# Sparsemax attention with a Fourier layer: the check of the thresholds is summed by rank on TensorE, ahead of the next keys

## What is computed

```
def sparsemax(x):
    zs = -jnp.sort(-x, axis=-1); cssv = jnp.cumsum(zs, axis=-1) - 1.0
    support = zs > cssv / rho
    k = jnp.maximum(jnp.sum(support, axis=-1, keepdims=True), 1)
    tau = jnp.take_along_axis(cssv, k - 1, axis=-1) / k
    return jnp.clip(x - tau, 0.0)
scores = jnp.einsum('bhqd,bhkd->bhqk', qh, kh) * scale
out = jnp.einsum('bhqk,bhkd->bhqd', sparsemax(scores), vh)
```

## Time and profile before

| | us |
|---|---|
| median of 3 runs | 724.58 |
| lowest and highest of them | 724.3, 726.02 |
| the profiled execution, its own time | 725.45 |
| its span, first to last instruction | 723.7 |
| TensorE busy (matmuls) | 584.8 |
| VectorE busy | 609.3 |
| ScalarE busy | 380.7 |
| GpSimd busy | 187.1 |

### The profile page before, as it was taken

One profiled execution on the slowest core, in us unless ns is written; L12 is line 12 of the kernel. 1 busy time (PEld: TensorE's weight loads), 2 busy tenths in 40 slices (PEclk: granted clock), 3 DMA queues, 4 the chain that ended last, 5 costly groups with the idle time before them and its releaser, 6 DMA issues.

```text
span 723.7 us, 14347 instructions
## 1 busy us (share of the span) xinstructions
PE 584.8 (81%) x4560; PEld 332.5 (46%) x4560; DVE 609.3 (84%) x2964; ACT 380.7 (53%) x657; POOL 187.1 (26%) x239
## 2 busy tenths in 40 slices
PE   3785989798814998899899998990889988997575
PEld 1343545454402654565455544550445544655242
DVE  5699799977966999999999999994899999999600
ACT  3664565766611755666566646560456665563321
POOL 2511403241220240415033502351014430301301
PEclk9879978999965999999999999996899999996857
DMA  9752131202220113130303030303102111200000
GB/s 315 237 166 72 27 103 47 59 0 71 68 76 0 28 28 101 33 84 15 110 26 95 6 105 28 106 1 84 42 1 78 39 45 31 59 17 14 11 1 11
DMA packets 33471, 44.23 MB, mean 61 GB/s; under 512 B 8353, under 2 KB 26785, under 8 KB 33382
## 3 DMA queue, kind: packets, MB, share of 16 engines
q1 hardware_dynamic: 32332, 41.16, 20.0%
q10 hardware_dynamic: 1056, 2.10, 0.8%
HBM read 23.77 MB, written 1.64 MB: 35 GB/s over the span
## 4 chain that ended last, share of the span: by engine, by line
PE 64%; issue 16%; ACT 11%; DVE 4%; SPq 3%; DMA 1%; POOL 1%; POOLq 0%; DVEq 0%
PE ring L456 33%; PE ring L522 8%; PE ring L545 5%; PE ring L599 5%; PE mix_bank L570 5%; PE ring L495 4%; PE ring L507 3%; ACT qst L674 2%; ACT S L674 2%; SPq L248 2%; ACT ctx L674 1%; DMA S<-in_L_xattn_Wk 1%; SPq L252 1%; ACT v L674 1%; ACT ks L682 1%
## 5 line engine op out<-in xcount | busy, mean ns | idle before, releaser
L929 DVE MAX8 cand<-S 100x8 f32<-100x45 f32 (+1 forms) x2048 | 223.1, 188 | 0.5 <-issue 0.4
L456 PE MATMUL ring<-wv,ctx 128*121 128x512 f16 x576 | 156.7, 392 | 0.0
L456 PE MATMUL ring<-ctx,wk 128*128 128x361 f16 x768 | 136.1, 339 | 4.5 <-DVE ctx L1108 4.5
L798 ACT ACTIVATE pT<-ring 121x800 f32<-121x800 f32 x96 | 80.5, 839 | 75.2 <-PE ring L599 75.2
L674 ACT ACTIVATE S<-ring 100x722 f32<-100x722 f32 x128 | 95.2, 774 | 27.6 <-PE ring L545 27.2
L456 PEld LDWEIGHTS ring<-ctx,wk 128*128 128x128 f16 x768 | 78.9, 104 | 58.6 <-issue 14.9
L333 POOL TENSOR_TENSOR ctx<-ctx_f,ctx 128x484 f16<-128x484 f32 x42 | 50.6, 1205 | 163.8 <-ACT ctx L674 163.4
L545 PE MATMUL ring<-kst,qst 96*100 96x361 f16 x256 | 68.0, 361 | 29.4 <-ACT S L674 12.9
L456 PEld LDWEIGHTS ring<-wv,ctx 128*121 128x121 f16 x576 | 71.8, 137 | 33.4 <-issue 7.9
L599 PEld LDWEIGHTS ring<-qst,kst 99*121 99x121 f16 x768 | 61.5, 150 | 45.5 <-issue 21.7
L341 POOL TENSOR_TENSOR ks<-k_f,ks 128x361 f16<-128x361 f32 x64 | 57.2, 894 | 90.9 <-ACT k_f L686 88.2
(11 more groups left out here) (126 smaller groups left out, 727.3 us busy)
## 6 DMA issues: line engine op xcount, KB each, us to landing
kst<-ks SPq DMA_DIRECT2D x384, 45.1 KB, 1.9
ctx_f<-in_ctx SPq DMA_DIRECT2D x45, 242.0 KB, 2.9
xq<-in_x SPq DMA_DIRECT2D x8, 200.0 KB
xr<-in_x SPq DMA_DIRECT2D x8, 200.0 KB
out_y<-att SPq DMA_DIRECT2D x8, 200.0 KB
S<-in_L_xattn_Wk ACTq DMA_DIRECT2D x1, 1024.0 KB, 6.8
wq<-in_L_xattn_Wq ACTq DMA_DIRECT2D x1, 1024.0 KB, 11.3
wcos<-in_L_ffn_theta SPq DMA_DIRECT2D x1, 1024.0 KB, 10.4
```

The lines of the kernel that those rows point to most:

```text
L456: last = nc.tensor.matmul(psum, lhs(c, i), w(c, j), start=(c == 0 and n == 0), stop=(c == DC - 1 and n == 2))
L798: nc.scalar.activation(pT[0:CK, u % 3, :, :], src, ACT.Relu).then_inc(two_read, 1)
L929: last = nc.vector.max(cand[:, h, 8 * n:8 * n + 8], S[0:L, HH * (i % 2) + h, cuts[n]:cuts[n + 1]])
```

## The change

It changes how the flags are made, where they are summed, and how they are read.

- `thresholds`: the last step is held at zero or above, so that counts can't rise; the five instructions of lines 969 to 979 are replaced by one comparison of all 8 x 16 x 8 candidates with tau, written to `over` by rank (16-bit, the ranks 128 elements apart).
- `sum_flags`: nine matmuls in place of two: `n_over` times ones, and for each rank its 128 marks times -1 (ranks one to seven) or +1 (the eighth), into 8 x 17 places of partition 0. It stands behind `scores(i+1)` in phase i, in even phases ahead of `o_of(b-1)`, no longer between the key groups of phase i+1.
- `read_flags` for `rank_flags`: a sum over the 17 places of each head, a comparison times 2^h, and a sum to one word; behind three heads in place of four. `settle` stands behind four heads in place of five, loads the word once, and finds the flagged heads by shifts and tests in three nested loops of two.
- the first `maxes` of a half waits for `flag_ready` of the half before.

```diff
-                pe.wait_ge(flag_ready, i + 1)
-                nc.tensor.matmul(flag_ps, ones[:, :], n_over[:, :], start=True, stop=False)
-                nc.tensor.matmul(flag_ps, minus[:, :], n_now[:, :], start=False, stop=True).then_inc(flag_sum, 1)
+                pe.wait_ge(flag_ready, i + 1)
+                nc.tensor.matmul(flag_ps[:, :, PIECES], ones[:, :], n_over[:, :], start=True, stop=True)
+                for r in range(8):
+                    last = nc.tensor.matmul(flag_ps[:, :, 0:PIECES], (one_b if r == 7 else minus_b)[:, :],
+                                            by_rank[:, r, :, :], start=(r == 0), stop=(r == 7))
+                last.then_inc(flag_sum, 1)
...
                         run(k_of(b + 1, 0, 0), 4)
                         run(k_of(b + 1, 1, 0), 4)
-                    if attended:
-                        sum_flags(i - 1)
...
                     weave(heads, fill, 1)
+                    if i < NH:
+                        sum_flags(i)
                     if b > 0:
                         run(o_of(b - 1), 4)
...
             def maxes(i, h):
                 dve.wait_ge(two_read, seen2(("s", i, h)))
+                if h == 0 and i > 0:
+                    dve.wait_ge(flag_ready, i)
...
+                nc.vector.scalar_tensor_tensor(t, step_t[:, :], 0.0, t, ALU.max, ALU.add).then_inc(tau_ready, 1)
                 dve.wait_ge(tau_ready, i + 1)
-                counted(nc.vector.tensor_tensor(marks[:, :, :, 7:8], pieces[:, :, :, 7:8],
-                                                t4.broadcast_to([L, HH, PIECES, 1]), ALU.is_lt))
...
+                nc.vector.tensor_tensor(by_rank.rearrange("p r g n -> p g n r"), pieces, t4.broadcast_to([L, HH, PIECES, 8]), ALU.is_ge).then_inc(flag_ready, 1)
...
+                nc.vector.reduce_sum(lost[:, :], flag_ps, AX).then_inc(check_step, 1)
+                dve.wait_ge(check_step, 1)
+                nc.vector.scalar_tensor_tensor(code[:, :], lost[:, :], 0.5, bit_c[:, :],
                                                ALU.is_gt, ALU.mult).then_inc(check_step, 1)
...
+                    nc.vector.reduce_sum(word_i[:, :], code[:, :], AX).then_inc(check_step, 1)
...
-                    with dve.Fori(0, HH // 2) as pair:
-                        leading = dve.value_load(ranked_i[0:1, bass.ds(2 * pair, 1)], min_val=0, max_val=HH)
...
+                    with dve.Fori(0, 2) as four:
+                        with dve.If(((word >> (4 * four)) & 15) > 0):
+                            with dve.Fori(0, 2) as pair:
+                                with dve.If(((word >> (4 * four + 2 * pair)) & 3) > 0):
+                                    with dve.Fori(0, 2) as k:
+                                        with dve.If(((word >> (4 * four + 2 * pair + k)) & 1) > 0):
+                                            refine(i, 4 * four + 2 * pair + k)
...
                     found = maxes(i, h)
+                    if h == 2 and i > 0:
+                        read_flags(i - 1)
                     if h == 3 and i > 0:
-                        rank_flags(i - 1)
-                    if h == 4 and i > 0:
                         settle(i - 1)
```

More of the change, by code:

```diff
@@ L148, in build_kernel @@
         dif, over = sb("dif", [L, HH, NCAND]), sb("over", [L, HH, NCAND], BF16)
-        fold = sb("fold", [L, HH, 2 + NCAND // 2], BF16)
+        fold = sb("fold", [L, HH, 2 + PIECES * max(RANKS) // 2], BF16)
         tau = sb("tau", [L, 2, HH])
[L151 to L154, removed]
+        f_sum, step_t, n_over = (sb(n, [L, HH]) for n in ("f_sum", "step_t", "n_over"))
+        zero = sb("zero", [L, 1])
+        one_b, minus_b = sb("one_b", [L, 1], BF16), sb("minus_b", [L, 1], BF16)
+        bit_c, code, lost = (sb(n, [1, HH]) for n in ("bit_c", "code", "lost"))
+        word_i = sb("word_i", [1, 1], I32)
         again, againT = sb("again", [P, 32]), sb("againT", [P, 32])
@@ L164, in build_kernel @@
         mask_row = over[:, :, :].rearrange("p g n -> p (g n)")[:, 0:N]
+        by_rank = over[:, :, :].rearrange("p g n -> p (g n)").rearrange("p (r g n) -> p r g n", r=8, g=HH)
         s_flat = S[:, :, :].rearrange("p h n -> p (h n)")
@@ L962, in thresholds @@
                     after(n)
-                    last = nc.vector.scalar_tensor_tensor(t, step_t[:, :], STRETCH[turn], t, ALU.mult, ALU.add)
                     if turn < len(RANKS) - 1:
-                        n = counted(last)
-                last.then_inc(tau_ready, 1)
+                        n = counted(nc.vector.scalar_tensor_tensor(t, step_t[:, :], STRETCH[turn], t, ALU.mult, ALU.add))
+                nc.vector.scalar_tensor_tensor(t, step_t[:, :], 0.0, t, ALU.max, ALU.add).then_inc(tau_ready, 1)
                 dve.wait_ge(tau_ready, i + 1)
-                marks = over[:, :, :].rearrange("p g (n r) -> p g n r", r=8)
-                counted(nc.vector.tensor_tensor(marks[:, :, :, 7:8], pieces[:, :, :, 7:8],
-                                                t4.broadcast_to([L, HH, PIECES, 1]), ALU.is_lt))
[L971 to L980, removed]
+                nc.vector.tensor_tensor(by_rank.rearrange("p r g n -> p g n r"), pieces, t4.broadcast_to([L, HH, PIECES, 8]), ALU.is_ge).then_inc(flag_ready, 1)
             def two_steps(t):
@@ L1012, in test_sums, with refine @@
                 dve.wait_ge(fix, 3 + P // 32)
-            def refine(i, number):
-                number = nc.s_assert_within(number, 1, HH, skip_runtime_bounds_check_because="inside If(number > 0)")
-                t = tau[:, i % 2, bass.ds(number - 1, 1)]
-                row = S[0:L, bass.ds(number - 1 + HH * (i % 2), 1), :].rearrange("p a n -> p (a n)")
+            def refine(i, h):
+                h = nc.s_assert_within(h, 0, HH - 1, skip_runtime_bounds_check_because="a sum of three bits")
+                t = tau[:, i % 2, bass.ds(h, 1)]
+                row = S[0:L, bass.ds(h + HH * (i % 2), 1), :].rearrange("p a n -> p (a n)")
                 dve.sem_clear(fix)
@@ L1052, in rank_flags @@
                                                ALU.is_gt, ALU.mult).then_inc(check_step, 1)
-                dve.wait_ge(check_step, 1)
-                nc.vector.max(ranked[:, :], code[:, :]).then_inc(check_step, 1)
                 dve.wait_ge(check_step, 2)
-                nc.vector.tensor_copy(ranked_i[:, :], ranked[:, :]).then_inc(check_step, 1)
+                with nc.allow_low_precision(reason="a sum of distinct powers of two under 256"):
+                    nc.vector.reduce_sum(word_i[:, :], code[:, :], AX).then_inc(check_step, 1)
@@ L1058, in settle @@
             def settle(i):
                 dve.wait_ge(check_step, 3)
[L1060 to L1061 removed]
+                word = dve.value_load(word_i[0:1, 0:1], min_val=0, max_val=2 ** HH - 1)
+                with dve.If(word < 1):
                     dve.sem_inc(verified, 1)
[L1063 removed]
+                with dve.If(word > 0):
                     dve.wait_ge(tau_split, i + 1)
[L1065 to L1071 removed]
+                    with dve.Fori(0, 2) as four:
[5 more added lines that the diff above has]
+                                            refine(i, 4 * four + 2 * pair + k)
```

25 lines of the change are left out of this document (9 added, 16 removed).

## The result

| | before | after |
|---|---|---|
| median, us (4 runs each, same chip) | 724.44 | 755.40 |
| lowest and highest | 722.93, 726.02 | 755.08, 756.05 |
| span of the profiled execution | 723.7 | 753.3 |

The ratio is 1.0428, 95% interval 1.0405 to 1.0452: **31 us slower**, far outside my range (721.5 to 731.0).

The account below looks back on a forecast made before the run. The prediction took TensorE to set the pace, with GpSimd's split close behind. Its terms, from +4.1 for the sum to -3.6 and -1.8 for finding heads, summed to +2.0 us on 724.58: 726.6, range 721.5 to 731.0.

Parts of the forecast that it names:

- VectorE's marks: In thresholds, one comparison of 1024 elements takes 1.9 us, with the new wait 1.95 in place of 3.18; almost none shows.
- s: VectorE's time saved per half by the new comparison: 1.2 us, between 0.8 and 1.7.
- B: Rival: slower, TensorE stands in front of the keys in every even half; 730.7 us at a 3.0 us comparison; chance 0.14.
- The place: Sum ahead of the keys: a new TensorE wait in half 4, +2.2 us, and +0.84 at the end.
- added nothing: Slow first keys after odd phases at low granted clock: flags take some of this stretch in place of keys, 0 us.
- TensorE's sum: Nine matmuls in place of two on TensorE: 0.37 us more per half, in eleven halves +4.1.
- Finding the heads: Head tests in the refined halves, 0.6 us less each: -3.6 in half 10, -1.8 in half 3.
- One head earlier: Earlier reading and settling: nothing without refinement; -0.2 us in half 3, +0.84 in half 10, cut off by GpSimd's split.
- The end: Last halves: flags ahead of o_of(6) +0.84 us, VectorE's saving -1.2, the last sum +0.37.
- A: The forecast's own mechanism holds: 724.2 to 728.9 us; chance 0.62.
- C: Rival: faster, the nine matmuls cost TensorE next to nothing, -2.3 us; 723.3 or 721.5 with further savings; chance 0.19.
- D: Rival: the flagged set changes, a refined half costing 18 to 27 us; about 700 or 745 us; chance 0.05.

Follow-up runs that it names:

- added comparisons: The changed kernel with seven forms of the comparison added at its end, twice each; kernel 768.67 us in its one run.
- the two kernels with the 2.0 us comparison: The changed kernel with the comparison's loops turned, ranks outermost: 735.83 us with the sum at the new place, 727.11 us with it back between the key groups.
- the fastest: The kernel before with the word of bits and the flags read behind three heads, settled behind four; sum at its old place: 718.20 us, ratio 0.9923.
- the quick comparison: The changed kernel with only the comparison's loops turned, ranks outermost, so the same marks are written in runs: 735.83 us, ratio 1.0142.
- both undone: The changed kernel with the sum put back between the key groups and the comparison's ranks outermost, the rest kept: 727.11 us, ratio 1.0034.
- the doubled ones: The kernel with both undone, its eight matmuls by rank run twice in each half: 741.64 us, ratio 1.0227.

## Why the prediction was wrong, point by point

**The step that failed: VectorE's marks.** I put s = +1.2 us per half, between 0.8 and 1.7; it is 3.18 - 4.77 = **-1.6**. The row that could tell stood in the earlier trace rows: line 969 writes its marks singly, eight apart. I took its start to start, 0.35 us for 128, called the scaled 2.8 us too high, and gave line 971 its full 1.30. Both run into one another, and the start of the next instruction isn't the end of the last one's writes. The two together take 187.62 + 1.30 - 187.27 = 1.65 us; line 971's share at the pace of natural order (1.22 us per 1024) is 1.07; 0.58 is left for line 969, 4.5 ns per mark, as in the change. The added comparisons bear this out: the same 128 marks alone take 0.72 us there, of which 0.15 is fixed by the line through the three least times (an estimate; each form ran twice, and the shorter two took longer the first time). Its own duration, 0.73 us for 128, scales to 5.8, an upper bound that I hadn't used: I had kept 2.3 as the upper end of the range. The rule of the Trainium skill that the prediction names ("Advanced Engine Details and Errata", "SBUF Cachelines") spoke against the layout, and the trace agrees; I had let it cost 0.4.

**The rival that came true is B**, at 4.7 us in place of 3.0: TensorE stands in front of its next work. It was not every even half, as I had it (1, 3, 4, 7, 12, 13), I think because VectorE, late itself, and the slow keys shift against each other. By B's own rule, two savings less per even half without a wait, 4.7 us would have given some 4.0 in each of four halves and 2.8 twice: 748. Its mechanism would have been enough for three quarters of the loss; I gave it 0.14.

**The place was under-priced** even with quick marks: 8.1 us on the kernel before, 8.7 between the two kernels with the 2.0 us comparison, 11.4 on the fastest (5 to 10 at equal clock). Mine came to about 3. What I had set to nothing is the clock. I had seen that it is low behind odd phases, and "added nothing", since the flags would take some of the slow stretch in place of keys. They don't: with the quick comparison the eight matmuls of odd halves 1 to 13 come 102 to 106 ns apart at the new place and 58 at the old one, 3 us in sum, and the keys take 2 more in sum, not less. And with the sum at this place there are stretches at the lower level where there were none, in `attend` above all (14.0 to 17.1 us). On the kernel before, whose marks aren't quicker, the lower clock in `attend` is 4.1 of the 8 us and the waits in halves 4, 8 and 10 are 3.3.

**TensorE's sum** (0.84 with its hole, 0.37 more per half): near, at the full clock. From the hole to the next keys it takes 0.93 in half 0, with 59 ns per matmul against my 57; in the seven halves at the lower level it is 0.43 more; the page "TensorE: Matmul & The Clock Gate" of the Trainium skill, section "Back-to-back issue gap", has about 81 ns for such a stream, which this trace doesn't show. The kernel with both undone is 8.9 us above the fastest, where 16 times 0.44 (its 48 keys with the sum among them take 7.95 us against 7.51) gives 7.0. I had counted eleven halves.

**Finding the heads** (-5.4 in two halves): right in kind, too high. Alone it brings 3.9. In the changed kernel half 10 takes 15.7 us from the passing of its gate to the transposes, 18.9 before: -3.2 for my -3.6. Half 3 takes 28.0 and 28.4: -0.4 for my -1.8; between its two refinements VectorE idles 3.8 us where it was 2.4. I take this for more tests than I had put; I didn't count them.

**One head earlier** (nothing, since GpSimd's split cuts it off): right, also with the sum at its old place, where the refinements of halves 3 and 10 start no sooner behind the split with it than without.

**The end** (0.84 - 1.2 + 0.37): -1.2 has the wrong sign with s, and TensorE's last wait is 8.06 us for 5.34. **A** fell with s; **C** had the matmuls at next to nothing, and the doubled ones show each of them on the path; **D**: three refinements as before, in the same two halves, so as many heads are flagged.

**What I had named as signs** spoke at once: TensorE waits for marks in more halves than 4 and 15 (B), VectorE's wait for the root is up by 13 us (I had 8, for the opposite reason), its busy time went up and not down. Two halves in the middle are 3.1 us longer (384.11 - 306.12 = 78.0 from keys to keys, 74.9 before); with both undone it is 0.75 (371.30 - 295.69), close to my 0.8.

One reading in the prediction was wrong and changed nothing: VectorE's longest wait is not the one for the square root but 22.5 us, once, near the end, for x1 from GpSimd.

## What to carry to other kernels

Cost a new layout by the narrowest row that writes in that way, by its own duration as well as by the start of the next instruction, and let the range reach to both: here the pace of 16-bit writes in a row was a quarter of the price. A wait in a stream that sets the pace is worth its slack: two groups of other work in front of it hid nearly all of 2.7 us more for the marks; without them they cost 19.6 us. And separate the parts of a change before judging it: the kernel with the decoding and the earlier reading alone is 6 us faster than the one before, mostly by the decoding, and the other parts buried this under 37. And compare runs at equal granted clock before giving a difference of 2 us to an edit.

## What was unexpected, and what stays open

- Single 16-bit writes of VectorE cost 4.6 ns each (4.70 us for 1024), whether 256 or, by the 128 marks in 0.72 us, 16 bytes apart. Over 1.22 us in a row that is 3.5 more, five times the extra of single 32-bit ones (1.92).
- Matmuls of 128 columns that read 16-bit marks in steps of 16 bytes take 226 ns each from start to start, at either level of the clock; where the marks lie in a row it is 59 at the full clock and 106 at the lower level.
- 0.46 us more on TensorE per half cost 0.9, and one kernel's runs lie 8 us apart with the clock granted. Which hole brings the lower level in which stretch isn't settled: the doubled kernel has no new hole and has it too, and the kernel before has it in the keys behind all odd phases but one (behind the scores of half 4 they take 7.83 us at full clock). I tried nothing that separates this from the shift of the engines against each other.
- Whether 32-bit marks by rank (1.92 us) at the old place would do better than the two comparisons and the folding wasn't tried; with the matmuls on the path there is little to gain.
